# Query halves and softmax sums moved by DMA, and value products two key tiles at a time, in an attention and mixture-of-experts kernel

## The reference

```python
xn = layernorm(layernorm(x)) * g1 + b1
q = xn @ Wq                          # 16 heads of 64
k, v = split(xn @ Wkv, 2)            # one head, shared
sim = einsum("hid,jd->hij", q * 64 ** -0.5, k)
attn = softmax(sim)
x = x + layernorm(einsum("hij,jd->hid", attn, v) @ Wo) * g2 + b2
h = layernorm(x)
top2, w = top_k(softmax(h @ gate_w.T), 2)          # normed to sum 1
x = x + sum over the two: w * (up(h) * gelu(gate(h))) @ down
```

## Time and profile before

| | |
|---|---|
| time, median of three | 622.52 us (621.23 to 623.45) |
| span of the profiled execution, first to last instruction | 619.0 us |
| PE busy | 576.5 us, 93% |
| DVE busy | 419.2 us, 68% |
| POOL busy | 394.9 us, 64% |
| ACT busy | 303.0 us, 49% |
| attention with its ramp | from 0 to about 467 us |
| experts | from there to the end |
| mean granted clock of TensorE | 0.981 |

### The profile page before, as it was taken

One profiled execution on the slowest core, in us unless ns is written; L12 is line 12 of the kernel. 1 busy time (PEld: TensorE's weight loads), 2 busy tenths in 40 slices (PEclk: granted clock), 3 DMA queues, 4 the chain that ended last, 5 costly groups with the idle time before them and its releaser, 6 DMA issues. The chain is left out here.

```text
span 619.0 us, 8823 instructions
## 1 busy us (share of the span) xinstructions
PE 576.5 (93%) x2611; PEld 328.8 (53%) x2611; DVE 419.2 (68%) x816; ACT 303.0 (49%) x568; POOL 394.9 (64%) x326
## 2 busy tenths in 40 slices
PE   8899999999999999989999988999998869999980
PEld 6455454454554454445544534444443558888870
DVE  4976659658747978875587789877487468444433
ACT  2345645355555554454656434455636453555530
POOL 5357667658668855698597558859746934454330
PEclk9999999999999999889999999999999999999995
DMA  6111011010101100070000000000006101230005
GB/s 177 69 70 70 25 48 69 1 69 6 65 28 43 71 1 2 4 272 32 2 0 2 1 2 18 18 1 1 9 2 191 46 22 32 66 92 27 26 11 203
DMA packets 23981, 29.29 MB, mean 47 GB/s; under 512 B 4403, under 2 KB 14901, under 8 KB 23936
## 3 DMA queue, kind: packets, MB, share of 16 engines
q1 hardware_dynamic: 21664, 24.50, 12.1%
q0 software_dynamic: 2272, 4.24, 2.0%
HBM read 13.73 MB, written 15.32 MB: 47 GB/s over the span
## 5 line engine op out<-in xcount | busy, mean ns | idle before, releaser
L1095 ACT ACTIVATE prob<-s_ps 128x512 f32<-128x512 f32 x256 | 150.5, 598 | 183.0 <-PE s_ps L1201 181.0
L1019 DVE TENSOR_REDUCE rowmax<-max_ps 128x1 f32<-128x512 f32 x256 | 173.1, 685 | 81.6 <-PE max_ps L1170 79.5
L950 POOL TENSOR_TENSOR fold<-prob 128x1024 f32<-128x1024 f32 x63 | 149.6, 2374 | 95.2 <-ACT prob L1095 94.7
L1215 PE MATMUL pv_ps<-prob,v 128*64 128x512 f32 x512 | 139.1, 623 | 0.0
L1199 PE MATMUL s_ps<-q_hl,khh 128*128 128x512 f32 x256 | 118.0, 461 | 0.6 <-ACT prob L1095 0.6
L1170 PE MATMUL max_ps<-khh,q_hl 128*128 128x512 f32 x256 | 103.6, 410 | 6.5 <-DVE q_hl L1008 3.3
L1201 PE MATMUL s_ps<-q_hm,kly 65*128 65x512 f32 x256 | 102.1, 399 | 0.0
L1199 PEld LDWEIGHTS s_ps<-q_hl,khh 128*128 128x128 f32 x256 | 48.6, 190 | 79.2 <-ACT prob L1095 59.8
L956 POOL TENSOR_TENSOR psums<-fold 128x512 f32<-128x512 f32 x63 | 81.7, 1296 | 4.9
L1170 PEld LDWEIGHTS max_ps<-khh,q_hl 128*128 128x128 f32 x256 | 49.1, 192 | 26.5 <-DVE rowmax L1019 9.4
L1201 PEld LDWEIGHTS s_ps<-q_hm,kly 65*128 65x128 f32 x256 | 48.8, 191 | 9.0 <-issue 3.4
(11 more groups left out here) (227 smaller groups left out, 783.2 us busy)
## 6 DMA issues: line engine op xcount, KB each, us to landing
sorted_rows<-raw_w SPq DMA_DIRECT2D x36, 260.0 KB, 2.6
raw_w<-in_gate_upT SPq DMA_DIRECT2D x8, 512.0 KB, 7.5
wd<-in_downT SPq DMA_DIRECT2D x8, 256.0 KB, 3.6
raw_w<-parts SPq DMA_DIRECT2D x8, 256.0 KB, 4.6
psums<-sorted_rows SPq DMA_DIRECT2D x22, 65.0 KB, 1.8
x<-in_x SPq DMA_DIRECT2D x4, 256.0 KB, 5.8
out<-x SPq DMA_DIRECT2D x4, 256.0 KB, 2.5
xs_first<-sorted_rows SPq DMA_DIRECT2D x15, 65.0 KB, 2.2
```

The costliest lines, as they stand in the source:

```text
L950: nc.gpsimd.tensor_tensor(fold[:, :, :], prob[:, head % 4, 0:2, :], prob[:, head % 4, 2:4, :], ALU.add).then_inc(prob_folded, 1)
L1019: nc.vector.tensor_reduce(rowmax[:, group % 2, it, i:i + 1], max_ps[:, k % 2, :], AX_X, ALU.max).then_inc(max_done, 1)
L1095: nc.scalar.activation(prob[:, head % 4, jt, :], s_ps[:, k % 2, :], ACT.Exp, scale=SCALE).then_inc(exp_done, 1)
L1215: last = nc.tensor.matmul(pv_ps[DH * hd:DH * hd + DH, :], v[:, b % 2, jt, :], prob[:, head % 4, jt, :], start=(jt == 0), stop=(jt == JT - 1))
```

## The change

It does four things. **Value products** come two key tiles at a time, at slots 7 and 11 of a pair, and behind the products Q and NORM of the same slot; SUM stands behind them. **Query halves** (from the sixth pair on) are made whole: ACT copies 128 partitions at once into `qh`, DVE subtracts once into `ql`, and SP moves the halves to the slots of `q_hl` and `q_hm` by six DMAs (step QMOVE), eight slots earlier than before; POOL's copy is gone. There is one `qh` and one `ql`, so the next pair's halves wait until the DMAs have landed. **Sums**: ACT copies `sum_ps` to `sums` (step SUMS), SP spreads its eight useful rows over 128 partitions of 32 (SPREAD, two DMAs in pieces of 128 bytes), DVE takes reciprocals and halves of those, and SP gathers them back into `rhl` (GATHER, two DMAs). **NORM** then reads 40 partitions instead of 128. Besides, `mrow` lies in a free part of `q_hm`, two constants are loaded otherwise, and the last row tiles share a semaphore by pairs.

```diff
-PV_AT = (6, 8, 9, 11)
+PV_AT = (7, 7, 11, 11)
-NORM_AT = (14, 17, 19, 22)
+NORM_AT = (15, 19, 21, 23)
-SUM_AT = (-7, 5)
+SUM_AT = (-5, 7)
+RECIP_STEPS = ("SUMS", "SPREAD", "RECIP", "GATHER")
+RECIP_AT = (8, 8, 11, 11)
+FIRST_Q_AT = (-3, 3, 7, 13)
+DIRECT = 5
...
-        at = (-30, -11, *FIRST_Q_AT)[pair] if pair < 4 else 8 * pair - 19 - lead
+        at = (-30, -11, *FIRST_Q_AT)[pair] if pair < DIRECT + 1 else 8 * pair - 27 - lead
...
+            for n, kind in enumerate(("Q", "QHI", "QLO", "QMOVE")):
+                place(at, 1.5 + 0.1 * n, kind, u, p)
...
             if kind == "RECIP":
-                last = nc.vector.reciprocal(rinv[:, quarter], sum_ps[:, quarter])
+                dve.wait_ge(spread_in, 32 * (u + 1))
+                link(dve, nc.vector.reciprocal(rinv[:, :], spread[:, :]))
...
+        def tail_sync(sp, kind, u):
+            if kind == "SPREAD":
+                sp.wait_ge(sums_copied, u + 1)
+                if u >= 1:
+                    sp.wait_ge(recip_done, u)
+                for half in range(2):
+                    sp.dma_start(spread[half * P // 2:(half + 1) * P // 2, :],
+                                 sums[half:P:32, :]).then_inc(spread_in, 16)
+            if kind == "GATHER":
+                sp.wait_ge(recip_done, u + 1)
...
+                for part in range(2):
+                    sp.dma_start(rhl[part * LOW_ROW:part * LOW_ROW + UH, :].bitcast(F32),
+                                 halves[:, part, :].bitcast(F32)).then_inc(rhl_in, 16)
+
         def tail_scalar(act, kind, u, a):
+            if kind == "SUMS":
+                act.wait_ge(sum_mm, 2 * (u + 1))
...
+                nc.scalar.activation(sums[:, :], sum_ps[:, :], ACT.Copy).then_inc(sums_copied, 1)
...
-                pe.wait_ge(recip_done, u + 1)
+                pe.wait_ge(rhl_in, 32 * (u + 1))
...
-                nc.tensor.matmul(sum_ps[:, :], headsel[:, a, :], rhl[:, :], start=True,
+                nc.tensor.matmul(sum_ps[:, :], headsel[0:LOW_ROW + UH, a, :], rhl[0:LOW_ROW + UH, :], start=True,
...
+                    if kind == "QMOVE":
+                        sp.wait_ge(qh_made, k - DIRECT + 1)
...
+                            sp.dma_start(q_hl[0:DH, slot, :].bitcast(F32),
+                                         qh[held, :].bitcast(F32)).then_inc(q_in, 16)
+                        sp.wait_ge(ql_made, k - DIRECT + 1)
...
+                    if kind == "QLO" and u * UP + a >= DIRECT:
+                        dve.wait_ge(qh_made, k - DIRECT + 1)
...
+                        nc.vector.tensor_tensor(ql[:, :], q_ps[:, :], qh[:, :].bitcast(F32),
+                                                ALU.subtract).then_inc(ql_made, 1)
...
+                    if kind == "QHI" and u * UP + a >= DIRECT:
...
+                        if k > DIRECT:
+                            q_came(act, k - 1)
+                            q_top_came(act, k - 1)
+                        nc.scalar.activation(qh[:, :], q_ps[:, :], ACT.Copy).then_inc(qh_made, 1)
...
+                        elif it == 0 and i % 2 == 0:
+                            q_came(pe, u * UP + i // 2)
```

More of the change, by code:

```diff
@@ L23 @@
 RAW_SLOTS = 5
+SPREAD = 32
+LOW_ROW = 32
 def attention_schedule(units):
@@ L80, in attention_schedule @@
         if u < units - 1:
-            place(after + SUM_AT[0], 5, "SUM", u, 0)
-            place(after + SUM_AT[1], 5, "SUM", u, 1)
-            place(after + RECIP_AT[4], 5, "RSPLIT", u, 0)
+            place(after + SUM_AT[0], 2.5, "SUM", u, 0)
+            place(after + SUM_AT[1], 2.5, "SUM", u, 1)
+            for n, kind in enumerate(RECIP_STEPS):
+                place(after + RECIP_AT[n], 5, kind, u, 0)
             for c in range(UP):
-                place(after + RECIP_AT[c], 5, "RECIP", u, c)
-                place(after + NORM_AT[c], 5, "NORM", u, c)
+                place(after + NORM_AT[c], 1.5, "NORM", u, c)
                 place(after + NORM_AT[c] + OUT_LAG, 5, "OUT", u, c)
@@ L271, in bass_preln_mqa_moe_kernel @@
         headsel = sb(whole, "headsel", [P, UP, P], F32R)
-        rih = sb(whole, "rih", [P, S], F32R)
+        sums = sb(whole, "sums", [P, S])
+        spread = sb(whole, "spread", [P, SPREAD])
+        rinv = sb(whole, "rinv", [P, SPREAD])
+        halves = sb(whole, "halves", [P, 2, SPREAD], F32R)
         rhl = sb(whole, "rhl", [P, S], F32R)
-        low_rows = sb(whole, "low_rows", [P, 1])
         raw = sb(whole, "raw", [P, RAW_SLOTS, S])
         ao = sb(whole, "ao", [P, 2, S])
-        rinv = sb(whole, "rinv", [P, S])
         wof = sb(whole, "wof", [P, PAIRS, P])
@@ L321, in bass_preln_mqa_moe_kernel, with tile_in, tiles_with @@
         down_mm = sem("down_mm")
-        xs_in = [sem(f"xs_in{k}") for k in range(NT)]
+        xs_in = [sem(f"xs_in{k}") for k in range(FIRST_TILES)] + [sem(f"xs_pair{n}") for n in range((REST + 1) // 2)]
+        def tile_in(k):
+            return k if k < FIRST_TILES else FIRST_TILES + (k - FIRST_TILES) // 2
+        def tiles_with(k):
+            return sum(tile_in(n) == tile_in(k) for n in range(NT))
         count = {"dve": 0, "pool": 0, "ln": 0, "ln_pool": 0, "ln_dve": 0}
@@ L703, in tail_vector @@
             if kind == "RECIP":
-                quarter = slice(a * P, (a + 1) * P)
-                if a == 0:
-                    dve.wait_ge(sum_mm, 2 * (u + 1))
-                last = nc.vector.reciprocal(rinv[:, quarter], sum_ps[:, quarter])
-                if a == 3:
-                    link(dve, last)
-            if kind == "RSPLIT":
-                if u >= 1:
[L714 to L719, removed]
+                dve.wait_ge(spread_in, 32 * (u + 1))
+                link(dve, nc.vector.reciprocal(rinv[:, :], spread[:, :]))
+                if u >= 1:
+                    dve.wait_ge(rhl_in, 32 * u)
+                link(dve, nc.vector.tensor_copy(halves[:, 0, :], rinv[:, :]))
+                nc.vector.tensor_tensor(halves[:, 1, :], rinv[:, :], halves[:, 0, :].bitcast(F32),
+                                        ALU.subtract).then_inc(recip_done, 1)
             if kind == "NORM":
@@ L783, in bass_preln_mqa_moe_kernel @@
         last_pv = max(n for n, step in enumerate(steps) if step[0] == "PV")
-        tail_steps = [step for step in steps[last_pv:] if step[0] in ("RAW", "RECIP", "RSPLIT", "NORM", "OUT")]
+        tail_steps = [step for step in steps[last_pv:] if step[0] in ("RAW", *RECIP_STEPS, "NORM", "OUT")]
         assert all(step in tail_steps or step[0] in ("PV", "SUM") for step in steps[last_pv:])
@@ L855, in _ @@
                 sp.dma_start(wof[:, :, :], wo.rearrange("(c p) n -> p c n", p=P)).then_inc(wo_in, 16)
+                for half in range(2):
+                    for part in range(2):
+                        row = part * LOW_ROW + half * UH // 2
+                        sp.dma_start(hs_raw[row:row + UH // 2, :, :],
+                                     head_rows[half + 2 * part:P:32, :, :]).then_inc(hs_in, 16)
                 for b in range(1, NB):
@@ L1332, in load_down @@
                                  downT[e].rearrange("(c p) n -> p c n", p=P)).then_inc(wd_in, 16)
+                tail_sync(sp, "SPREAD", last_unit)
                 for k in range(EARLY_ROWS, LIST_TILES[0]):
+                    if k == EARLY_ROWS + 1:
+                        tail_sync(sp, "GATHER", last_unit)
                     if k - EARLY_ROWS < E // 2:
@@ L1410, in weigh @@
                                             ALU.mult).then_inc(eow_ready, 1)
-                for quarter in range(4):
-                    tail_vector(dve, "RECIP", last_unit, quarter)
-                tail_vector(dve, "RSPLIT", last_unit, 0)
+                tail_vector(dve, "RECIP", last_unit, 0)
                 low_gate_up(dve, 0, wl_ready)
```

102 lines of the change are left out of this document (71 added, 31 removed).

## The result

The changed kernel is slower: 647.3 us (median of four, 646.7 to 649.2) against 621.9 for the kernel before on the same chip, a ratio of 1.042 (95% interval 1.037 to 1.047). I had forecast 616.8 and a range that ended at 628.6; the prediction was wrong in its sign. The profiled execution has a span of 647.5 us, against 619.0.

What follows compares the result with a forecast made beforehand. PE, busy 93% of the span and issuing without data waits in the attention, was taken as the bound. Terms -20.8 -1.2 -8.6 -3.4 +7.8 +1.8 +13.3 +4.2 +1.2 = -5.7 took 622.5 to 616.8 us; range 602.5 to 628.6.

Steps and rivals of the forecast that it cites:

- steps 1 and 2: Value products in twos save ways in and out, 20.8 us off; SUM behind them shares the way, 1.2 off.
- step 7: GATHER on SP: NORM waits 2.5 us in three units, 0.6 in four, 9.9; with 3.4 of clock, 13.3 on.
- rival of the slow second hop: GATHER's landing takes 3.0 us instead of 1.8, giving 628.6; decides against the change from about 2.6; chance 0.18.
- steps 4 and 7: Half-clock stretches behind PE's waits: two old ones go, 3.4 us off; two come at NORM, 3.4 on.
- step 9: Ramp: the sixth and seventh pairs' halves share one qh, ACT is held 1.8 us; 1.2 on.
- step 3: PE's old attention waits, at NORM, for low halves and row maxima, go: 8.6 us off if nothing replaces them.
- DVE rival: Stretches of four slots: DVE 0.57 us late in half of 24, 6.8 together, 623.6 us; chance 0.10.
- Steps 5, 6 and 8: RAW on ACT delays exponentials, 7.8 us on; SUMS likewise, 1.8 on; NORM's narrow row tile, 4.2 on.
- step 5: RAW between first and second exponential delays the fourth slot's scores 0.25 us, 31 times: 7.8 on.
- Step 8: NORM as a 64-row tile: 0.09 in and 0.09 out 21 times, 0.33 seven times; 4.2 us on.

Runs made afterwards that it cites:

- e7: The changed kernel with GATHER's two DMAs ahead of the SHIFT's two and its fills in SP's order; 619.2 us.
- e2: The changed kernel with RAW ahead of the first exponential behind the value products instead of behind it; 646.4 us.
- e3: The kernel before with only the value products two key tiles at a time, at slots 7 and 11; 646.9 us against 618.2 beside it.
- e6: e1 with value products one key tile at a time again, at slots 6, 8, 9 and 11; 631.2 us.
- e1: The changed kernel with NORM four, two, two and two slots later and OUT three slots behind it instead of four; 618.2 us.
- e9: e5's kernel once more, timed against the kernel before; 613.4 us, median of four, ratio 0.984.
- e5: e1 with the sixth pair's queries at slot 10 instead of 13; 610.4 us.

## Why the prediction was wrong, step by step

**Right: what bounds the kernel, steps 1 and 2.** PE's issue time did bound it, and fell by 20.4 us for the 22.0 of these two steps (17.0 by the median distance). From the start of the product ahead of a double value product to the start of the one behind it pass 2.19 us, of which 0.24 is the product ahead; with the 0.10 of the way out that shows at the next score it costs 2.05, the 1.19 + 0.86 of the forecast.

**Right in place: the timetable of step 7.** PE in the first unit's tail of the changed kernel, from the second SUM over the double PV and the SHIFT to NORM:

```profile
102.08 0.50 PE L1289 MATMUL s_ps<-q_hl,khh 128*128 128x512 f32 x1
...
105.38 1.94 PE L1305 MATMUL pv_ps<-prob,v 128*64 128x512 f32 x8
107.24 0.60 PE L1264 MATMUL q_ps<-ident,rowmax 128*4 128x128 f32 x4
...
111.39 0.40 PE L1191 MATMUL q_ps<-xl,wqh 128*128 128x512 f32 x1
114.85 0.50 PE L802 MATMUL sum_ps<-rhl,headsel 40*128 40x512 f32 x1 [3.06 <-DMA rhl<-halves]
```

With T at 102.08 the SHIFT comes at T + 5.2 (forecast 5.1), SP's DMAs at 108.49, T + 6.4 (6.4), PE is ready for NORM at T + 9.7 (9.4), GATHER starts behind the fills at T + 9.7 (9.5). **Mis-sized: its last leg.** Two issues take 1.44 us for the 1.2 I had from other DMAs, and from the second one (half of 1.44 behind 111.76, 112.48) to NORM's start are 2.4 us where I took 1.8. So 3.06 instead of 2.5, and 1.0 instead of 0.6; with 1.94 in a unit for which I had 0.6, and no wait in the sixth, where PE had stood for row maxima just before, 13.1 instead of 9.9. The rival of the slow second hop, 3.0 us, was not it either: 2.4 lies below its point of decision. (GATHER is not the smallest transfer in the kernel, as I had argued against it: SPREAD moves 8 KB a piece and a SHIFT 4.)

**Wrong: the clock (steps 4 and 7).** This is the largest miss of a single term. I gave the old falls back once, 3.4 us, for NORM's waits, as if two short stretches were all that such waits could bring. In the changed kernel the clock falls eight times in the attention, for 3.4 to 6.8 us each; clock costs 16.7 us instead of 5.2. Three of the falls, at 168, 229 and 458 us, come with NORM's waits: three where I had charged two, each of 6.8 us where those before had 3.4, and some 9 us lost where I had 3.4. Four more stand behind waits that the forecast had at nothing or as too short: for row maxima (1.29 and 1.59 us, at 48 and 402 us), for an exponential (2.94, step 9) and for a SHIFT's rows (2.13). The eighth, at 468 us, has no wait above 0.3 us in the 9 us before it. e7 shows that most of this hangs on NORM: with the same work and the same order on PE, 14.3 us less of waits bring 13.5 us less of clock. Not every long wait does it, though: the 3.06 us at 111.78 is followed by full clock, and so were two waits of 1.5 and 1.6 us in the kernel before (at 364 and 385 us), which my rows did not show.

**Wrong: step 3, that the old waits go and nothing takes their place.** They did go: low halves from 3.0 to 0.3, long reciprocals altogether. But from 25 to 490 us there are 4.5 us for exponentials (2.9 of them step 9), 2.1 for a SHIFT's rows, 2.4 at Q for `kly` and one other DVE result, and 6.3 for row maxima (1.9 before). The longest of the last is 1.6 us behind DVE's stalled copy at 397.85. The next that the kernel before did not have is 1.29 us at 47.74, behind two low halves of a pair in the ramp:

```profile
45.46 1.41 DVE L1088 TENSOR_TENSOR q_hl<-q_ps,q_hl 64x512 fp32r<-64x512 f32 x2
```

I had named the DVE rival and given it 0.10 with a price of 6.8. Its waits for row maxima rose by 4.4: 1.3 by what I had named, other work of DVE between row maxima, 1.6 by something I had not, POOL holding up DVE; the rest are small, and no run tests either cause by itself. Together waits are 15.2 us above the forecast: 3.2 at NORM, 1.7 in the ramp, and some 10 that step 3 had at nothing.

**Wrong in size: step 9.** 2.9 us for 1.2, and one fall of the clock more. I counted SP's six issues and the landing, 5.3 us from the sixth pair's high half, but not what stands ahead of them in the same queue: the half was ready at 55.7, and the SHIFT's pair and four fills held SP until 56.65, 1.1 us. From the first issue to the seventh pair's copy then passed 5.9 us (56.76 to 62.68), 0.6 more than I had. The prediction had such fills in step 7 and forgot them here.

**Steps 5, 6 and 8** were of the right size together: 13.8 forecast, 17.2 in the table (13.5 by the median distance) with DVE's small delays in it. But e2 shows that step 5's cause was told too simply: with RAW in the other place the small stalls fall by 4.2 us and the waits rise by as much. It fits that the fourth slot's wait is the sum of what ACT has to do in four slots, and that where RAW stands only decides which exponential is late; no run tests that by itself. Step 8's price is real for row tiles, 0.19 to 0.31 us a NORM, and was mis-sized: 21 x 0.19 + 7 x 0.31 = 6.2 us for 4.2. The Trainium skill, "TensorEngine Tiling (Array Packing)", Key Properties, says that a change of the tiling mode drains TensorE; the rows agree, though they show the price and not the drain itself.

**Where the forecast's chances were.** Slower had 0.22, by two mechanisms that both were not the main one. Of the signs that I had named for being wrong, waits of several us for row maxima came (6.3); a landing of GATHER above 2.5 us and value products of 2.3 us did not (2.4 and 1.94). The step that failed first is the sum of 7: the waits at NORM and their place were right to about half a microsecond in most units, but I charged 13.3 us where 13.1 of waits and some 9 of clock came. The second is step 3, which put at nothing the waits that took the place of the old ones.

## What to carry to other kernels

A wait of one to three microseconds on TensorE in a dense stretch is to be charged for itself and again for the clock behind it, and as often as it occurs. How much again differed here: 17.7 us more of waits came with 11.5 of clock in the changed kernel, 14.3 less with 13.5 in e7, 19.6 more, in shorter pieces, with 6.1 in e3. When a result comes to go through a queue that waits in order, list what stands ahead of it there at each place, the start-up too, and give its consumer the slack of the whole list: four slots, or two DMAs put in another order, were worth 28 us here. Parts of a change that look separable may not be: value products in twos lose some 28 us where DVE still has its old work (e3), and gain 13 where it has not and NORM comes late enough (e6 against e1).

## What the runs showed of the hardware

- A DVE copy of 32 elements in each partition takes 0.18 to 0.30 us where POOL adds up no exponentials, and lasts until the end of such an addition where one runs (1.49, 2.60 us); a subtraction of two tiles does the same (0.19, and 1.34 or 2.22), a reciprocal doesn't (0.35 both ways). The Trainium skill, "SBUF — State Buffer", Who interferes with whom, has a port pair that DVE and GpSimd share: a copy can take it for a whole instruction, and an instruction with two inputs contends with GpSimd's reads. The rows beside POOL's additions agree.
- A product over 40 rows is slower than one over 128 where its neighbours are full: 0.77 us for 0.46 from the product ahead of it to the one behind. It is not the number of rows alone: the score product over 65 rows (L1291) between full ones starts 0.24 us behind the one ahead and 0.23 ahead of the next (114.26, 114.50, 114.73 in e9), as full ones do.
- From the second issue of a DMA of 16 KB in pieces of 128 bytes within the chip's own memory to the work that it releases pass 2.2 to 2.4 us, half a microsecond more than the 65 KB transfer of the earlier trace rows took to land.
- The clock fell to its lower level behind most single waits of 1.3 to 3 us, and not behind one of the longest (3.06 us). The same wait of 1.45 us for row maxima near 28 us was followed by a fall in the kernel before, e1 and e7, and by none in the changed kernel, e2 and e5; in e3 the clock fell at 104, 190 and 278 us beside waits of about 1.0 us and less. So the length of the single wait does not settle it, and what does stays open.
